# Three norms and a weight request in a twelve-part decoder kernel: norm steps as separate instructions, one norm moved out of an attention, one request moved into another

## What is computed

```python
x = x + L0_attn(layernorm(x))                      # part 0
x = x + L0_xattn(layernorm(x), ctx, mask)          # part 1: 16 heads, 512 keys
x = x + L0_ffn(layernorm(x))                       # part 2: shared expert + 32 routed, one choice
x = x + L1_attn(layernorm(x))                      # part 3: causal, clipped scores
x = x + L1_xattn(layernorm(x), ctx)                # part 4: every 16th key of ctx, "gathered"
x = x + L1_ffn(layernorm(x))                       # part 5: 8 experts, two choices
...                                                # parts 6 to 9
x = x + L3_xattn(layernorm(x), ctx, ctx, mask)     # part 10
x = x + L3_ffn(layernorm(x))                       # part 11: activations rounded to 8 bits, ternary weights

def _layernorm(x, axis=-1, eps=1e-05):
    m = jnp.mean(x, axis=axis, keepdims=True)
    v = jnp.var(x, axis=axis, keepdims=True)
    return (x - m) / jnp.sqrt(v + eps)

def _quant_act(x):                                 # in L3_ffn
    scale = 127.0 / jnp.clip(jnp.max(jnp.abs(x), axis=-1, keepdims=True), EPS, None)
    xq = jnp.clip(jnp.round(x * scale), -128.0, 127.0) / scale
```

## Time and profile before

| what | value |
|---|---|
| runs | 1433.00, 1439.01, 1435.27 us |
| median | 1435.27 us |
| the profiled execution's own time | 1451.29 us |
| its span on the core | 1449.4 us |
| mean granted TensorE clock | 0.89 of full speed |
| busy: TensorE, VectorE, ScalarE, GpSimd | 1181.9, 904.8, 705.8, 283.0 us |
| DMA | 114.33 MB, mean 79 GB/s |

### The profile page before, as it was taken

The page is one execution under the profiler, slowest core; times in us unless marked ns, Lnnn a source line. Parts: engine busy times, 40 slices in busy tenths (PEclk is TensorE's granted clock), DMA queues, the critical chain, the costliest instruction groups (busy, mean ns, idle before and its releaser), DMA issues. The chain is left out here.

```text
span 1449.4 us, 26598 instructions
## 1 busy us (share of the span) xinstructions
PE 1181.9 (82%) x9412; PEld 734.0 (51%) x9417; DVE 904.8 (62%) x2352; ACT 705.8 (49%) x1448; POOL 283.0 (20%) x567
## 2 busy tenths in 40 slices
PE   5888996785796497667999999999965778989994
PEld 2333334683342487355666666666645742333332
DVE  5768864335658354876766776776742056777866
ACT  3666881222633121213665666666632435646664
POOL 3422211352010264100000000000005514212210
PEclk8899997897789699776999999999987877999998
DMA  7321252794402576000000000000026625211200
GB/s 190 91 63 53 65 158 85 229 288 129 124 4 92 172 260 199 15 0 1 1 1 1 1 1 2 1 1 1 1 67 195 202 96 132 60 54 46 52 8 15
DMA packets 88036, 114.33 MB, mean 79 GB/s; under 512 B 11090, under 2 KB 68127, under 8 KB 87439
## 3 DMA queue, kind: packets, MB, share of 16 engines
q1 hardware_dynamic: 83458, 103.52, 24.1%
q0 software_dynamic: 4448, 9.12, 2.0%
HBM read 85.79 MB, written 25.82 MB: 77 GB/s over the span
## 5 line engine op out<-in xcount | busy, mean ns | idle before, releaser
L2721 DVE CUSTOM_DVE_ANT_0 wring<-ps,probs 128x768 f32<-128x768 f32 x128 | 122.6, 958 | 52.3 <-PE ps L2593 52.0
L1154 PE MATMUL ps<-probs,vaug 128*32 128x256 f32 (+1 forms) x1792 | 145.5, 400 | 11.6 <-ACT probs L1118 8.1
L2677 ACT COPY qs<-ps 128x768 f32<-128x768 f32 x128 | 102.4, 801 | 97.6 <-PE ps L2600 97.6
L278 POOL TENSOR_TENSOR rstd<-veps,mhalf 128x2 f32<-128x2 f32 (+2 forms) x30 | 28.0, 934 | 589.1 <-DVE veps L241 559.3
L1109 ACT ACTIVATE probs<-ps 128x512 f32<-128x512 f32 x192 | 104.2, 595 | 68.8 <-PE ps L954 68.6
L986 DVE TENSOR_REDUCE mx<-ps 128x2 f32<-128x1024 f32 (+1 forms) x96 | 115.5, 1220 | 19.7 <-PE ps L904 18.6
L1113 ACT ACTIVATE probs<-ps 128x512 f32<-128x512 f32 x192 | 104.8, 594 | 39.3 <-PE ps L1066 38.2
L2659 ACT ACTIVATE wring<-wring,r 128x768 f32<-128x768 f32 x128 | 120.7, 943 | 2.9 <-DVE r L2724 2.9
L2600 PE MATMUL ps<-ident,wring 128*128 128x128 f32 x768 | 110.2, 280 | 3.2 <-DVE wring L2764 3.2
L2600 PEld LDWEIGHTS ps<-ident,wring 128*128 128x128 f32 x768 | 84.4, 141 | 39.4 <-issue 35.3
L2018 POOL DMA_INDIRECT scr_y<-probs x85 | 83.1, 977 | 96.2 <-DVE probs L1972 79.7
(11 more groups left out here) (349 smaller groups left out, 2369.2 us busy)
## 6 DMA issues: line engine op xcount, KB each, us to landing
wring<-in_L_ffn_w SPq DMA_DIRECT2D x19, 768.0 KB
wring<-in_L_ffn_w SPq DMA_DIRECT2D x32, 384.0 KB
wring<-in_L_ffn_w SPq DMA_DIRECT2D x19, 514.0 KB
qs<-scr_q SPq DMA_DIRECT2D x18, 192.0 KB
qs<-scr_qx SPq DMA_DIRECT2D x16, 192.0 KB
probs<-in_L_ffn_w SPq DMA_DIRECT2D x8, 384.0 KB
probs<-in_L_ffn_w SPq DMA_DIRECT2D x4, 768.0 KB
scr_k<-probs SPq DMA_DIRECT2D x21, 128.0 KB, 2.9
```

What stands on the lines that cost most here:

```text
L1154: ins = pe.matmul(ps[32 * j:32 * j + 32, self.av_bank(s), q0:S], vaug[:, s % 2, kt, j, :], probs[:, s % 2, j, at:at + S - q0], start=(kt = ...
L2677: act.copy(self.pT[:, g % 2, j, :, k * P:(k + 1) * P], self.buffer("turn", i, 0, KV).rearrange("p (t n) -> p t n", n=P)).then_inc(self.out ...
L2721: dve.tensor_tensor_reduce(self.sc[:, s, :], src, self.maskb[:, u // (2 * PR), :], 1.0, -3.0e38, ALU.add, ALU.max, self.top[:, s:s + 1]).t ...
```

## The change

Norm 4 leaves the tails and is made in two halves of four tiles after L1_attn. In L0_xattn and L3_xattn the tail's measuring, scaling and rounding become single steps spread over the units or steps of the list; each instruction that others of VectorE need notes its count in `part_chain`, and the later step waits for that count. The power on GpSimd moves from "t_stats" to "t_var". In L3_xattn the transposes move from groups 7, 11 and 15 to groups 9, 13 and to the very end (behind the last "y"). The shared expert's weights are requested by SyncE in group 10 of L0_xattn.

```diff
-    by_batch = (1, 2, 4, 11, 13, 14)
-    tails = {1: 2, 2: 4, 4: 14}
+    by_batch = (1, 2, 11, 13, 14)
+    part_chain = {}
+    tails = {1: 2, 4: 14}
...
+    def stats_part_vector(dve, n, part):
+        at = tiles_of(n, part)
+        for j in range(at.start, at.stop):
+            ins = dve.bn_stats(stats[:, j, :], x[:, j, :])
+        ins.then_inc(dchain, 1)
+        chained[dchain.name] = chained.get(dchain.name, 0) + 1
+        part_chain["stats"] = chained[dchain.name]
+    def aggregate_part_vector(dve, n, part):
+        at = tiles_of(n, part)
+        dve.wait_ge(dchain, part_chain["stats"])
...
+    def variance_part_vector(dve, n, part):
+        dve.wait_ge(dchain, part_chain["aggr"])
+        dve.tensor_scalar(veps[:, at], mv[:, at, 1], EPS, None, ALU.add).then_inc(ln_var.sem, 1)
+    def scale_tile_vector(dve, n, part, t):
...
+            self.tail_at = 9 if self.tail == 14 else 7
...
         def turn_tail_tensor(self, pe, b, o):
-            if self.mask == "causal":
...
-            else:
-                pe.wait_ge(o_sb.sem, o_sb.at(self.n, o))
+            pe.wait_ge(o_sb.sem, o_sb.at(self.n, min(o, G)))
...
-            if self.tail and o >= 7 and o % 4 == 3:
-                yield "t_tp", (o - 7) // 4, o
+            if self.tail and o >= self.tail_at and (o - self.tail_at) % NQ == 0:
+                yield "t_tp", (o - self.tail_at) // NQ, o
...
+                if self.n == 1 and g == 10:
+                    mixtures[2].shared_sync(sp)
...
         # masked_steps (L3_xattn)
-                yield from self.tail_steps(t, 33, 16, {0: ("t_stats",), 3: ("t_h",), 5: ("t_q",)})
+                yield from self.tail_steps(t, 33, 16, {0: ("t_stats",), 1: ("t_aggr",), 2: ("t_var",), 5: ("t_h0",), 6: ("t_h1",), 7: ("t_big",),
+                                                      8: ("t_inv",), 9: ("t_scale",), 10: ("t_q0",), 11: ("t_q1",), 12: ("t_q2",)})
+                if t == (G + 1) * self.u + self.behind + self.u:
+                    yield "t_tp", 2, G
+                    yield "t_hT", 2, G
         # causal_steps (L1_attn)
-            if u == 1:
-                yield from self.tail_steps(s, 7, 4, {0: ("t_stats",), 1: ("t_h",), 2: ("t_tp", "t_hT")})
         # plain_steps (L0_xattn)
-                yield from self.tail_steps(s * self.u + u, 8 * self.u + 7, 4 * self.u, {0: ("t_stats",), 6: ("t_h",)})
+                yield from self.tail_steps(s * self.u + u, 8 * self.u + 7, 4 * self.u, {0: ("t_stats",), 1: ("t_aggr",), 2: ("t_var",), 6: ("t_h0",), 7: ("t_h1",)})
         # gpsimd_step
-            if what == "t_stats":
+            if what == "t_var":
                 power_gpsimd(pool, self.tail, s)
         # Mixture
+        def shared_sync(self, sp):
+            sp.dma_start(wslot[0][:, 0:self.packed.shape[2]], self.packed[0]).then_inc(w_in[0].sem, 16)
         # Gathered.tensor
-                if c:
-                    part_tensor(pe, self.norm, B - 1, 6, 0)
-                pe.wait_ge(*turned(self.norm, c))
+                pe.wait_ge(ln_hT.sem, ln_hT.at(self.norm, c + 1))
         # Ternary.tensor
             for t in range(4):
+                if t == 3:
+                    pe.wait_ge(ln_hT.sem, ln_hT.at(self.norm, B - 1))
                 self.up_tensor(pe, t)
```

More of the change, by code:

```diff
@@ L1429, in vector_step @@
             elif what == "t_stats":
[L1430 to L1434, removed]
+                dve.wait_ge(y_out.sem, y_out.at(self.n, s + 1))
+                stats_part_vector(dve, self.tail, s)
+            elif what == "t_aggr":
+                aggregate_part_vector(dve, self.tail, s)
+            elif what == "t_var":
+                variance_part_vector(dve, self.tail, s)
+            elif what in ("t_h0", "t_h1"):
+                dve.wait_ge(ln_tp.sem, ln_tp.at(self.norm, ln_tp.totals[self.norm]))
+                scale_tile_vector(dve, self.tail, s, int(what[3]))
+            elif what == "t_big":
+                others[11].big_vector(dve, s)
+            elif what == "t_inv":
+                others[11].inverse_vector(dve, s)
+            elif what == "t_scale":
+                others[11].scale_vector(dve, s)
+            elif what in ("t_q0", "t_q1"):
+                others[11].round_vector(dve, s, int(what[3]))
+            elif what == "t_q2":
+                others[11].integer_vector(dve, s)
         def scalar(self, act):
@@ L2145, in scalar @@
         def scalar(self, act):
-            part_scalar(act, self.norm, B - 1, 6, 0)
             for what, t in self.order():
@@ L2950, in out_vector, with mark @@
                                      in1=x[:, q, :], op0=ALU.mult, op1=ALU.add).then_inc(f_done.sem, 1)
-        def quantise_vector(self, dve, b):
-            at = slice(2 * b, 2 * b + 2)
-            dve.wait_ge(ln_h.sem, ln_h.at(made(self.norm), b + 1))
-            link(dve, dchain, dve.tensor_reduce(self.col(64 + 2 * b, 2), h[:, at, :], AX.X, ALU.max, apply_absolute_value=True))
-            self.scales_vector(dve, 64 + 2 * b, 72 + 2 * b, 16 + 2 * b, 2, 2)
-            for t in range(at.start, at.stop):
-                ins = dve.tensor_scalar(h[:, t, :], h[:, t, :], self.col(72 + t), ROUND, ALU.mult, ALU.add)
-            link(dve, dchain, ins)
-            dve.tensor_scalar(self.hi[:, at, :], h[:, at, :], ROUND, None, ALU.subtract).then_inc(f_q.sem, 1)
+        def mark(self, ins, what):
+            ins.then_inc(dchain, 1)
+            chained[dchain.name] += 1
+            part_chain[what] = chained[dchain.name]
@@ new lines, in big_vector, with inverse_vector @@
+        def big_vector(self, dve, b):
+            dve.wait_ge(ln_h.sem, ln_h.at(made(self.norm), b + 1))
+            self.mark(dve.tensor_reduce(self.col(64 + 2 * b, 2), h[:, 2 * b:2 * b + 2, :], AX.X, ALU.max, apply_absolute_value=True), "big")
+        def inverse_vector(self, dve, b):
+            big, inv = self.col(64 + 2 * b, 2), self.col(72 + 2 * b, 2)
+            dve.wait_ge(dchain, part_chain["big"])
+            link(dve, dchain, dve.tensor_scalar(big, big, EPS, None, ALU.max))
+            self.mark(dve.reciprocal(inv, big), "inv")
```

62 lines of the change are left out of this document (36 added, 26 removed).

## The result

The changed kernel takes 1421.99 us (median of ten runs, 1416.82 to 1427.87); the kernel before, beside it in ten runs, takes 1435.16 (1429.12 to 1440.43). The medians lie 13.2 us apart. The ratio on record, 0.9897 with a 95% interval of 0.9877 to 0.9917, puts the gain at 14.8 us, with 11.9 to 17.7 possible. The forecast was 13.1 less, 1422.2.

A forecast was written before the change was run, and what follows sets the result against it. TensorE was taken to set the pace, with its clock level and idle time before matmuls deciding. Terms −1.3 − 5.5 + 0.2 − 2.7 − 2.8 − 1.0 sum to −13.1: 1422.2 us on the median; own range 1418 to 1425, overall 1414 to 1430.

The forecast's parts named there:

- (c): Norm 4, L1_attn and head of L1_xattn: TensorE saves 0.6, VectorE's added norm work costs 0.8; net +0.2 us.
- (e): L3_xattn behind the second rounding block: TensorE's clock no longer falls once the idle time is gone; −2.8 us.
- (a): L0_xattn, norm 2's tail: GpSimd's power moves behind the split, removing a 0.65 us TensorE stall in two batch entries; −1.3 us.
- (b): Into L0_ffn: earlier weights' request removes 3.72 us idle and keeps the clock full 1.8 us longer; −5.5 us.
- (d): L3_xattn: rounding spread over single steps removes TensorE's idle time for the maxima behind two blocks; −2.7 us.
- (f): End of L3_xattn: sums and last osb no longer wait behind transposes and ScalarE's copy; −1.0 us, the moved work costing 0.
- over 11.5 is rival 3: Sign at L1_xattn's head: L2094 starting over 11.5 us after context_tensor's start means norm 4 is exposed in full.
- rival 3: Head of L1_xattn: norm 4 exposed in full, +2.9 in place of +0.2; total −10.4, 1424.9 us; chance 0.08.
- Rival 4: L3_xattn and L0_xattn: single steps gain nothing, small delays add up to the old stalls; −6.3, 1429.0 us; chance 0.06.
- Rival 1: L3_xattn: the clock falls anyway, there or a batch entry on; 2.8 us not won, −10.3, 1425.0 us; chance 0.25.
- Rival 6: Above all expert stages: shifted against the clock, more time at its lower level, slower at 1442.5 us and over; chance 0.03.

The follow-up runs named there:

- experiment 5: Changed kernel with norm 4 again a tail of L1_attn, in blocks; ratio to the kernel before 0.9884 (0.9831 to 0.9938).
- experiment 6: Kernel before, unchanged, profiled once more for L3_xattn's second rounding block; the entry behind that block took 30.88 us, against 32.28 in the first profile.
- g1: Changed kernel with norm 2's measuring in one block, GpSimd's power ahead of the split again; L0_xattn's two middle batch entries take 24.71 and 24.35 us.
- g2: Changed kernel with norm 2's measuring in one block, but the power behind GpSimd's split; L0_xattn's two middle batch entries take 23.88 and 23.52 us.
- g4: Kernel before with three filler matmuls on old data ahead of the wait for the shared expert's weights; ratio 0.9958 (0.9929 to 0.9986), 6.0 us less.
- f1: Kernel before with the early request for the shared expert's weights as its only change; ratio 0.9963 (0.9934 to 0.9992), 5.4 us less.
- f2: Changed kernel with the weights' request late again, all else kept; ratio to the kernel before 0.9907 (0.9874 to 0.994), 13.5 us below it.
- experiment 2: Kernel before with filler matmuls on old data ahead of the wait for the weights; ratio 0.9994 with seven, 0.9958 with three.

## Why the prediction was right, point by point

The total fell on the forecast, and that is luck in part: two terms, (c) and (e), were off by 2.3 and 1.4 us in opposite directions, and the 13.2 of the medians, which it hit to 0.1, stands beside 14.8 by the ratio. Means over the profiles that have a piece of code against those that don't:

| step | forecast | measured | from |
|---|---|---|---|
| (a) L0_xattn | −1.3 | −1.6 | 0.80 + 0.83 |
| (b) to the copy | −5.5 | −5.7 | 10.8 (3 profiles) to 5.1 (8) |
| (b) beyond it | 0 | −0.5, not shown | 16.9 (3) to 16.4 (8) |
| (c) norm 4 | +0.2 | −2.1; +0.2 at an equal clock | experiment 5 |
| (d) rounding | −2.7 | −2.3 | 2 x 1.17 |
| (e) clock behind it | −2.8 | −1.4 | experiment 6 |
| (f) end; L3_ffn | −1.0; 0 | −1.1; −0.1 | 18.1 (5) to 17.0 (8); 25.79 to 25.66 |

The sum of the measured column is −14.8, or −14.3 without the one that is not shown, within the 11.9 to 17.7 of the timed runs.

- **(a)** Cause and place shown by g1 against g2. The size was taken from the idle time of 0.65 alone; the group is shorter by 0.83.
- **(b)** The weights' landing is shown by g4, in which the DMA is named, and by f1 and f2. That the clock has a part is shown too, its size only as 1.3 to 3.3 us (experiment 2). The assumption that the clock falls about two microseconds into the stretch was wrong in place: with TensorE busy it is either full (4.53 to 4.66) or low at the start and full later (5.5 to 5.7); it was at its lower level all through in none of eight profiles. The forecast had the copy 6.0 us behind x (228.1 in the profile of before); the mean is 5.1. The term still came out right, because it was taken off the 11.53 of one profile, and the mean of the three is 10.8. The half microsecond in the stretch behind the copy rests on one profile of before (17.85); the two others with the late request lie within the new ones' range.
- **(c)** The step that failed is the clock. I priced instructions and covers, and their net was right at an equal clock, by two errors of 0.4 that cancel (L1_attn −1.0 where I had −0.6, head +1.2 where I had +0.8). But I left out that with the tail the clock falls earlier at the end of L1_attn and comes back later behind it. The sentence "over 11.5 is rival 3" settles that one: the values' matmuls start 8.8 behind `context_tensor`'s start, which is also less than the 9 to 10 I had named, since `context_tensor` takes 5.33 us there and not 6.18.
- **(d)** Right in mechanism, 0.2 short for each block: the transposes that moved to group 9 and 13 lengthen the step with the y from 2.11 to 2.31. I had priced the moved transposes for the third entry only. Rival 4 falls: no idle time for mx is left.
- **(e)** Mis-sized: 2.8 was one execution's value, the mean of five is 1.4. Rival 1, that the fall comes anyway, is half right: the fall is a matter of chance, but in seven profiles without the stall it didn't come elsewhere. The Trainium skill's word, cited in (e), that the number of slow matmuls varies from run to run is said there of a kernel's start; the trace agrees for the middle of this one, with 0 to 2.8 us for the same code.
- **(f)** Right to 0.1 us; the cover of the moved transposes held, with 0.5 us of slack.
- Rival 6 didn't come about as a cost of the change, but its price is real: unchanged expert stages differ by 13.5 us between the two profiles. The prediction named this as a sign of being wrong (over 3 us in stages without a changed line), and the sign came. It speaks against holding the two spans together and not against the steps: L2_ffn, where 9.9 of the 13.5 us lie, takes 105 to 108 us on one chip and 93 to 96 on the other whatever the code. The timed runs and the stretches are what the forecast is judged by.
- The slices were misread in one point: the earlier trace rows has digits of 6 and 7 at about 580 to 690 us as well. No term rests on it.

What stays open: why one chip is 20 us slower than the other, why the clock falls ahead of the last x of part 1 in some profiles and not in others, and why the last piece of L0_ffn took 96.9 us in f2. None of these was tried.

## What to carry to other kernels

Read an idle time together with the clock of what follows it: here a late 384 KB transfer cost 3.7 us of waiting and another 1.3 to 3.3 because TensorE's clock, with the engine left idle, came back later (6 to 16 us behind x instead of under 3). Three matmuls of filler alone brought the copy about half as far forward as the early request did. See whether the clock had fallen before the idle time began, as it had in two of the three profiles. When a small instruction of a shared queue (one GpSimd power) stands ahead of something that TensorE waits for, move it behind, and leave the engine with slack alone. And take several profiles before pricing a fall of the clock: the same code had it at 0, 1.4 and 2.8 us. Note the chip with each profile.

## What the runs showed that I had not expected

- The reason "issue" can be a DMA: the same wait is named "issue" with 3.72 and 3.84 us, and "DMA wring<-in_L_ffn_w" once there was work just ahead of it and 1.34 us of it were left.
- Taking three pairs of short transposes and VectorE's tail out of L1_attn keeps the clock at 1.00 to its last x in all seven profiles (with them it falls before that in six of six, if only by hundredths in one), although TensorE has less to do by it, not more: busy 7.01 of 8.89 us against 7.70 of 9.54.
- Paced stretches repeat to 0.04 us over 13 profiles, while L2_ffn, with the same code, takes 93 to 96 us in four profiles on one chip and 105 to 108 in seven on another. A change of 1 us can be shown in the first kind and not by any time of the whole.
